# Latent attentions with scores taken on the latent keys and an output projection in split format

## The reference

```
q_c = rmsnorm(h @ w_qa, g_qa)                     # 128 tokens x 192
q = (q_c @ w_qb) -> 32 heads x (128 + 64)         # q_nope, q_rope
kv = h @ w_kva;  k_c, k_rope = kv[:64], kv[64:]   # 64 latent values, 64 rotary values
k_c = rmsnorm(k_c, g_kva)
k_nope, v = (k_c @ w_kvb) -> 32 heads x (128 + 128)
q_rope, k_rope = rotary(q_rope), rotary(k_rope)   # k_rope is the same for all heads
scores = ([q_nope, q_rope] . [k_nope, k_rope]) * (128 + 64) ** -0.5
out = concat_heads(softmax(scores) @ v) @ w_o     # 4096 x 512
```

## Time and profile before

| | us |
|---|---|
| median of 3 executions | 1812.53 |
| lowest, highest | 1809.76, 1815.47 |
| the profiled execution, its own time | 1815.04 |
| its span, first to last instruction | 1813.2 |

### The profile page before, as it was taken

One profiled execution on the slowest core, in us unless ns is written; L12 is line 12 of the kernel. 1 busy time (PEld: TensorE's weight loads), 2 busy tenths in 40 slices (PEclk: granted clock), 3 DMA queues, 4 the chain that ended last, 5 costly groups with the idle time before them and its releaser, 6 DMA issues. The chain is left out here.

```text
span 1813.2 us, 23109 instructions
## 1 busy us (share of the span) xinstructions
PE 1622.6 (89%) x7617; PEld 1207.7 (67%) x7617; DVE 1071.5 (59%) x2144; ACT 890.5 (49%) x1528; POOL 207.4 (11%) x186
## 2 busy tenths in 40 slices
PE   5999999999987568797899987978999999999995
PEld 4778877887853233574666655756777777877873
DVE  5566666576649941443478844435665665575473
ACT  4554555455444311232188862326565565565552
POOL 0000000000013500000156640000000000000000
PEclk9999999999999868899999988999999999999997
DMA  7010011101090033253342103532010010010011
GB/s 265 1 58 35 27 54 54 39 23 58 2 361 24 0 157 92 79 168 116 71 87 38 27 7 114 168 142 113 1 59 35 23 58 35 31 50 35 23 54 73
DMA packets 30248, 129.51 MB, mean 71 GB/s; under 512 B 4929, under 2 KB 7105, under 8 KB 21489
## 3 DMA queue, kind: packets, MB, share of 16 engines
q1 hardware_dynamic: 30192, 128.84, 21.5%
HBM read 123.06 MB, written 0.26 MB: 68 GB/s over the span
## 5 line engine op out<-in xcount | busy, mean ns | idle before, releaser
L1871 POOL TENSOR_TENSOR L2x_p_lo<-L2x_e_t,L2x_p_hi 128x512 fp32r<-128x512 f32 x80 | 105.1, 1325 | 62.8 <-ACT L2x_p_hi L2056 61.9
L746 DVE TENSOR_TENSOR L0x_k_lo<-bank,L0x_k_hi 128x512 fp32r<-128x512 f32 x128 | 85.7, 689 | 42.6 <-ACT L0x_k_hi L635 42.2
L746 DVE TENSOR_TENSOR L3x_k_lo<-bank,L3x_k_hi 128x512 fp32r<-128x512 f32 x128 | 85.5, 689 | 40.0 <-ACT L3x_k_hi L635 39.8
L389 PE MATMUL bank<-L0x_ctx_hi,L0x_w_hi 128*128 128x512 f32 x256 | 103.7, 405 | 4.2 <-DVE L0x_ctx_lo L661 4.2
L389 PE MATMUL bank<-L3x_ctx_hi,L3x_w_hi 128*128 128x512 f32 x256 | 102.9, 402 | 4.2 <-DVE L3x_ctx_lo L661 4.2
L390 PE MATMUL bank<-L3x_ctx_lo,L3x_w_hi 128*128 128x512 f32 x256 | 101.2, 395 | 0.0
L635 ACT ACTIVATE L0x_k_hi<-bank 128x512 fp32r<-128x512 f32 x128 | 74.2, 599 | 54.8 <-PE bank L511 54.8
L391 PE MATMUL bank<-L0x_ctx_hi,L0x_w_lo 128*128 128x512 f32 x256 | 101.1, 395 | 0.0
L391 PE MATMUL bank<-L3x_ctx_hi,L3x_w_lo 128*128 128x512 f32 x256 | 100.9, 394 | 0.0
L635 ACT ACTIVATE L3x_k_hi<-bank 128x512 fp32r<-128x512 f32 x128 | 74.0, 599 | 53.9 <-PE bank L511 53.9
L390 PE MATMUL bank<-L0x_ctx_lo,L0x_w_hi 128*128 128x512 f32 x256 | 100.3, 392 | 0.0
(11 more groups left out here) (618 smaller groups left out, 4229.8 us busy)
## 6 DMA issues: line engine op xcount, KB each, us to landing
L0x_w_kqv<-in_L0x_kqv SPq DMA_DIRECT2D x7, 1536.0 KB, 6.3
L3x_w_kqv<-in_L3x_kqv SPq DMA_DIRECT2D x7, 1536.0 KB, 6.3
L0x_w_o<-in_L0x_o SPq DMA_DIRECT2D x8, 1024.0 KB, 4.9
L1a_w_o<-in_L1a_o SPq DMA_DIRECT2D x8, 1024.0 KB, 4.8
L2a_w_o<-in_L2a_o SPq DMA_DIRECT2D x8, 1024.0 KB, 5.0
L3x_w_o<-in_L3x_o SPq DMA_DIRECT2D x8, 1024.0 KB, 4.9
L0x_s<-in_ctx_t SPq DMA_DIRECT2D x4, 1024.0 KB, 12.2
L0a_w<-in_L0a_w SPq DMA_DIRECT2D x4, 1024.0 KB, 10.9
```

Of the source, the lines that this page charges most:

```text
L389: pe.matmul(out, left[0], right[0], start=start, stop=False)
L746: dve.tensor_tensor(p_lo[:, kt % 4, :], ring_bank(kt)[:], bits(p_hi[:, kt % 4, :]), ALU.subtract).then_inc(p_ready, 1)
L1871: pool.tensor_tensor(p_lo[:, t % 8, :], e_of(t), bits(p_hi[:, t % 8, :]), ALU.subtract).then_inc(low_pool, 1)
```

## The change

Scores. The key projection is gone. Instead each head's query (128 rows) is multiplied by that head's key weights (`w_kb`, a new tile, 128 rows by the 64 latents, written twice side by side), `absorb`, L2325's place taken by matmuls into bank 1; the result's 64 rows and the 64 rows of the turned rotary queries are copied into one tile `qk_t` of 128 rows, and the score is one matmul per head against `kc_t`, which holds the 64 key latents and the 64 rotary key values. So that the copies stay in their own rows, even heads have latents first and odd heads rotary first; `kc_t` exists in both orders.

Output projection. The values weighed are kept as `o_hi` (fp32r, by ScalarE) and `o_lo` (the rest, by VectorE); the weights as `wo_hi` (ScalarE, `split_high`, four copies per group) and `wo_lo` (GpSimd, `split_low`, four subtractions per group). For each head three fp32r matmuls replace one in full fp32. All groups add up in bank 4; x is added to once, at the end. The addition into x in each step and its wait go.

Order. On TensorE the value projection comes behind weighing, then the rotary transposes (now into the free half of bank 3), then `absorb`, then the output projection. On VectorE `o_lo` comes behind the rotary addition, then the copies of the turned and the absorbed halves, and the probabilities' multiplication last. On ScalarE `split_high(g+1)` comes last in a step and waits for `project_out(g-1)`. The load of w_o waits for `wo_lo` two groups back instead of for the projection.

```diff
+                sp.dma_start(w_kb[b][:], a["kb"][b]).then_inc(w_in[b], 16)
...
+                def split_low(g, b):
+                    for h in range(HG):
+                        pool.wait_ge(wo_hi_ready, g * 4 + h + 1)
+                        pool.tensor_tensor(wo_lo[b][:, h, :], w_o[b][:, h, :], bits(wo_hi[b][:, h, :]),
+                                           ALU.subtract).then_inc(wo_lo_ready, 1)
...
                 def load_output(n, b):
-                    sp.wait_ge(wo_done, n - 1)
+                    sp.wait_ge(wo_lo_ready, n * 4 - 4)
...
-                    pe.wait_ge(k_copied, g + 1)
-                    for h in range(HG):
-                        mm = pe.matmul(banks[1][:, h * P:(h + 1) * P], w_lo[b][:, KO + h * HD:KO + (h + 1) * HD],
-                                       lat_lo[:, 1, :], start=True, stop=True)
-                    mm.then_inc(k_proj, 1)
...
+                def absorb(g, b):
+
+                    pe.wait_ge(q_copied, g + 2)
+                    pe.wait_ge(qk_copied, g + 1)
+                    for h in range(HG):
+                        mm = pe.matmul(banks[1][:, h * P:(h + 1) * P], w_kb[b][:, h, :], q_t[:, h, :],
+                                       start=True, stop=True)
+                    mm.then_inc(absorbed, 1)
+
                 def score(g):
...
-                        pe.matmul(banks[5][:, h * P:(h + 1) * P], q_t[:, h, :], k_t[:, h, :], start=True, stop=False)
-                        mm = pe.matmul(banks[5][:, h * P:(h + 1) * P], q_pe_t[:, h, :], lat_lo[:, 2, :],
-                                       start=False, stop=True)
+                        mm = pe.matmul(banks[5][:, h * P:(h + 1) * P], qk_t[:, h, :], kc_t[:, h % 2, :], start=True,
+                                       stop=True)
...
+                def project_out(g, b, first=False, last=False):
+                    pe.wait_ge(o_lo_ready, g + 2)
+                    pe.wait_ge(wo_lo_ready, g * 4 + 4)
                     for h in range(HG):
-                        mm = pe.matmul(banks[6][:], o_t[:, h, :], w_o[b][:, h, :], start=(h == 0),
-                                       stop=(h == HG - 1))
+                        pe.matmul(wo_bank[:], o_hi[:, h, :], wo_hi[b][:, h, :], start=(first and h == 0), stop=False)
+                        pe.matmul(wo_bank[:], o_hi[:, h, :], wo_lo[b][:, h, :], start=False, stop=False)
+                        mm = pe.matmul(wo_bank[:], o_lo[:, h, :], wo_hi[b][:, h, :], start=False,
+                                       stop=(last and h == HG - 1))
...
                     if after:
+                        project_v(g + 1, 1 - b)
                         turn_rotary(g + 1)
+                        absorb(g + 1, 1 - b)
                     if before:
-                        project_out(g - 1, 1 - b, prev_i)
+                        project_out(g - 1, 1 - b, first, last)
...
+                def split_high(g, b, i, used=True):
+                    act.wait_ge(o_in[b], i * 16 + 16)
+                    if used:
+                        act.wait_ge(wo_done, g - 1)
+                    for h in range(HG):
+                        act.activation(wo_hi[b][:, h, :], w_o[b][:, h, :], ACT.Copy).then_inc(wo_hi_ready, 1)
...
                     if after:
                         keep_v(g + 1, 1 - b, used=before)
+                    if before and further:
+                        split_high(g + 1, 1 - b, i)
...
                     if after:
-                        keep(g + 1)
+                        keep_rotary(g + 1)
+                    if before:
+                        dve.wait_ge(o_hi_ready, g)
+                        dve.tensor_tensor(o_lo[:], per_head(banks[7]), bits(o_hi[:]), ALU.subtract).then_inc(o_lo_ready, 1)
+                    if after:
+                        keep_turned(g + 1)
+                        keep_absorbed(g + 1)
...
-                    if before:
-                        dve.wait_ge(wo_done, g)
-                        dve.tensor_tensor(core.x[:], core.x[:], banks[6][:], ALU.add).then_inc(x_added, 1)
...
+                dve.wait_ge(wo_done, NG)
+                dve.tensor_tensor(core.x[:], core.x[:], wo_bank[:], ALU.add)
```

More of the change, by code:

```diff
@@ L2224, in latent_attention @@
         p_t = st.sb("p_t", [P, HG, P])
-        o_t = st.sb("o_t", [P, HG, P])
+        o_hi = st.sb("o_hi", [P, HG, P], F32R)
+        o_lo = st.sb("o_lo", [P, HG, P], F32R)
+        wo_hi = [st.sb(f"wo_hi{b}", [P, HG, D], F32R) for b in range(2)]
+        wo_lo = [st.sb(f"wo_lo{b}", [P, HG, D], F32R) for b in range(2)]
         own = st.sem("own")
@@ L2399, in _ @@
                 step(NG - 1, 1, NG // 2 - 1, after=False)
-                step(NG, 0, NG // 2, this=False, after=False)
+                step(NG, 0, NG // 2, this=False, after=False, last=True)
             @block.scalar
@@ L2415, in _, with keep_q @@
                 act.activation(rstd[:, 1:2], sumsq[:, 1:2], ACT.Sqrt, bias=bias, scale=1.0 / KR).then_inc(rms_ready, 1)
-                def keep_q(g):
+                def keep_q(g, used=True):
                     act.wait_ge(q_proj, g + 1)
-                    if not (isinstance(g, int) and g == 0):
-                        act.wait_ge(s_ready, g)
+                    if used:
+                        act.wait_ge(absorbed, g)
                     act.activation(q_t[:], per_head(banks[0]), ACT.Copy).then_inc(q_copied, 1)
@@ L2427, in keep_v, with step @@
                     act.activation(v_sb[b][:], per_head(banks[2]), ACT.Copy).then_inc(v_copied, 1)
-                def step(g, b, before=True, this=True, after=True):
+                def step(g, b, i, before=True, this=True, after=True, further=True):
                     if before:
                         act.wait_ge(p_turned, g)
+                        if not (isinstance(g, int) and g == 1):
+                            act.wait_ge(o_ready, g - 1)
                         act.activation(p_t[:], per_head(banks[6]), ACT.Copy).then_inc(p_t_ready, 1)
@@ L2441, in step @@
                         act.wait_ge(o_ready, g)
-                        act.activation(o_t[:], per_head(banks[7]), ACT.Copy).then_inc(o_t_ready, 1)
+                        if not (isinstance(g, int) and g == 1):
+                            act.wait_ge(wo_done, g - 1)
+                        act.activation(o_hi[:], per_head(banks[7]), ACT.Copy).then_inc(o_hi_ready, 1)
                     if after:
                         keep_v(g + 1, 1 - b, used=before)
-                keep_q(0)
+                    if before and further:
+                        split_high(g + 1, 1 - b, i)
+                keep_q(0, used=False)
+                split_high(0, 0, 0, used=False)
                 keep_v(0, 0, used=False)
-                step(0, 0, before=False)
-                with act.Fori(0, NG // 2 - 1) as i:
-                    step(i * 2 + 1, 1)
-                    step(i * 2 + 2, 0)
-                step(NG - 1, 1, after=False)
-                step(NG, 0, this=False, after=False)
+                step(0, 0, 0, before=False)
+                split_high(1, 1, 0, used=False)
+                step(1, 1, 1)
+                step(2, 0, 1)
+                with act.Fori(1, NG // 2 - 1) as i:
+                    step(i * 2 + 1, 1, i + 1)
+                    step(i * 2 + 2, 0, i + 1)
+                step(NG - 1, 1, 0, after=False, further=False)
+                step(NG, 0, 0, this=False, after=False, further=False)
             @block.vector
@@ L2476, in _ @@
-                steps.then(dve.tensor_tensor(k_sw[:, 0:half], src[:, half:], rot[:, 1, 0:half], ALU.mult))
+                dve.scalar_tensor_tensor(lat[:], banks[0][:, 0:QR], rstd[:, 0:1], row_sb[:, 0:QR],
+                                         ALU.mult, ALU.mult)
+                for order in range(2):
+                    dve.scalar_tensor_tensor(kc[:, order, order * KR:(order + 1) * KR], banks[0][:, QR:QR + KR],
+                                             rstd[:, 1:2], row_sb[:, QR:], ALU.mult, ALU.mult)
@@ L2484, in keep, with keep_rotary @@
+                def keep_rotary(g, used=True):
                     dve.wait_ge(pe_proj, g + 1)
[L2485 removed]
+                    if used:
                         dve.wait_ge(pe_turned, g)
[L2487 to L2488 removed]
+                    wide, thin = [P, HG // 2, RD], [P, HG // 2, half]
                     cos = rot[:, 0, :].unsqueeze(1).to_broadcast(wide)
@@ L2510, in turn_rotary, with keep_absorbed @@
                     copy.then_inc(pe_copied, 1)
+                def keep_absorbed(g):
+                    dve.wait_ge(absorbed, g + 1)
+                    for odd in range(2):
+                        rows = slice(odd * RD, (odd + 1) * RD)
+                        copy = dve.tensor_copy(qk_t[rows, odd:HG:2, :], per_head(banks[1])[rows, odd:HG:2, :])
+                    copy.then_inc(qk_copied, 1)
                 def step(g, b, before=True, this=True, after=True):
```

140 lines of the change are left out of this document (74 added, 66 removed).

## The result

| | before, us | after, us |
|---|---|---|
| median (lowest to highest), 4 runs each | 1811.78 (1809.76 to 1815.47) | **1780.89** (1777.76 to 1782.18) |
| profiled execution, its own time | 1815.04 | 1777.76 |
| its span | 1813.2 | 1776.0 |
| mean granted TensorE clock | 0.955 | 0.958 |

The ratio is 0.9824, with an interval of 0.981 to 0.9838: the change makes the kernel 1.8% faster, 30.9 us. The forecast was 1782. The changed kernel was timed twice more, five executions each time, against before on the same chip: 1776.93 (0.9817, interval 0.9794 to 0.984) and 1776.6 (0.9811, 0.9787 to 0.9834).

What follows compares the result with a forecast made beforehand. TensorE was taken as the bound, its steady step falling 2.31 us to 9.65. Steady steps 27.7, first steps 0.8, tails 3.0 and clock -1.0 sum to 30.5 us off: median 1782, range 1769 to 1797.

Steps and rivals of the forecast that it cites:

- Output projection: TensorE, each step: 4 full fp32 matmuls become 12 fp32r passes taking 2.75 us, 0.78 less.
- The gap: TensorE ahead of the output projection: 0.7 us of waiting and issue goes, as o_hi and o_lo are hidden.
- The ring: Closed chain from projection through ScalarE's split, exponentials, o_hi and o_lo to projection: 9.15 us, 0.45 to spare, cost 0.
- Rival A: The ring through ScalarE is the bound: 0.5 to 1 us more a step, 1791 us; chance 0.18.
- GpSimd's hold: VectorE's rotary addition held at worst for one GpSimd instruction, 1.33 us: 0 in steady steps, 0.6 in each stage's first.
- Rival C: VectorE is kept out for GpSimd's whole run: step 10.6 us, at 6 us held 13.8 and 1834 in all; chance 0.05.
- First step: First to second score in each latent stage: 8.11 us becomes 7.0 to 7.1, gain 1.0 minus 0.6 for the hold.
- Tail: Eighth score to the end of the last addition into x: 16.25 us against 17.78, 1.5 less per stage.
- clock -0.5 a stage: Tails of both latent stages: 0.5 us lost in each to TensorE's lower clock, bounds -1.7 to +2.75.
- Preparation: Ahead of the first score: key projection goes, absorb and its copies come, 0 within 1 us per stage.
- Rival B: TensorE's sum as forecast, edges free, L1a's clock regained, passes at 0.221 us: 1777 us; chance 0.17 with the forecast's scatter.
- D: The change does not do what it says: within 5 us of the time before; chance 0.03.

Runs made afterwards that it cites:

- e1: Changed kernel with the output projection back in full fp32, without the split of weights and values: 1781.02 us, run again 1782.17 us.
- e3: Changed kernel with the value projection back ahead of weighing on TensorE: 1791.39 us (one execution).
- e4: Two runs of the changed kernel, with one or two more ScalarE copies of 128x512 behind each group's four: 1788.46 and 1786.11 us (one execution each).
- e5: Changed kernel with GpSimd's four subtractions per group cut from 128x512 to 128x4: 1774.86 us, ratio 0.9799.
- e8: Kernel before the change, with all groups added up in one PSUM bank and x added to once at the end: 1815.46 us (one execution).
- e4_act_plus2: Changed kernel with two more ScalarE copies of 128x512 behind the four of each group: 1786.11 us (one execution).
- e6: Changed kernel with GpSimd's four subtractions of 128x512 issued as one of 128x2048: 1797.39 us, ratio 0.9905.
- e7: Changed kernel with ScalarE's order changed in the last steps and VectorE's multiplication moved earlier in the first step: 1777.54 us, ratio 0.9801.
- e2: Changed kernel with every score matmul issued twice: 1793.64 us (one execution).

## Why the prediction was right, step by step

- *The bound.* TensorE's sum, right: doubling the scores lengthened the step by exactly their 0.90. Forecast 9.65 with the edges, measured 9.62 in L1a. In L2a the six steps came to 9.81 on average (1095.71 to 1154.54), because of the late second step.
- *Scores.* 0.89 less, right (773.10 to 773.99). Keys for absorb, 0: right within 0.01 (absorb 0.90 in e1).
- *Output projection.* 2.75 forecast; absorb and projection take 3.66, less 0.90 is 2.76. Right. Its gain was split wrongly: 0.67 by e1, not 0.78, because 3.53 held 0.10 of restart after the wait. The removed gap is worth that much more, 0.8 instead of 0.7. The sum of both is the same.
- *The gap.* Hidden, right: no wait in steady steps, and e3 brings 0.62 of it back. The chain from weighing to the projection was put at 1.6 of 1.98, a spare of 0.38; e3 gives 0.24.
- *The ring.* 9.15 with 0.45 of slack, right by e4. That the sum fits so closely is in part luck: in the step shown the exponentials take 1.54 (1.64 forecast), the output projection behind its short wait 2.87 (2.75), and the rest differs by less than 0.1. Rival A (the ring is the bound) is excluded, by a margin of less than one copy.
- *GpSimd's hold.* "Until that one instruction has ended": right for both lengths. The addition ends 0.28 us behind the end of one subtraction in both, and takes 1.54 beside instructions of 1.28 and 3.87 beside one of 4.52. Rival C (kept out for the whole run) is excluded: held to the end of the four (779.24) and 0.28 more, the addition would have taken 2.9. The step's cost of 0 was right (e5). The 0.6 per stage for the held multiplication was the mean of a thing that either does not happen or costs 1.16 us in the step behind it. The SBUF page of the Trainium skill ("SBUF — State Buffer", section "Who interferes with whom") says that a VectorE instruction with two SBUF inputs contends with a GpSimd instruction that reads SBUF, and calls the shared ports an exclusive lock. The traces agree: the addition of 0.43 took 3.87 beside the subtraction of 4.52, which had started 0.93 ahead of it.
- *First step.* 7.0 to 7.1 forecast, 6.94 and 6.93 measured: right.
- *Tail.* 16.25 forecast, 16.16 in L1a (811.53 to 827.69), right. In L2a 17.76, of which 1.6 is the stretch at the lower clock. The term "clock -0.5 a stage" was 0 in L1a, and L1a gave back the 1.7 that before had lost there (-3.3 instead of -1.5), which the sum had not counted; in L2a it was 1.6. A mean of 0.5 stood for a cost that is there or not.
- *Preparation.* 0 within 1: 0.3 and 0.7 gained, within the bound; e8 shows that the stretch in L2a moves by 1.1 without a change of its code. *DMA.* w_o landed in 7.1 us, not 4.8, beside more traffic; nothing waited for it.
- *Sum.* Steady steps 26.9 (27.7 forecast), first steps 2.35 (2.0, less 1.2 for the hold, which is in the steady steps here), tails 3.3 (3.0 less 1.0 for the clock), preparation 1.0 (0): 33.6 against 30.5. The terms that were too small are L1a's tail and the preparation (1.3 and 1.0), and the steps by 0.7 together. The medians of the three timings are 30.9, 33.8 and 35.2 us below before's on the same chip; the forecast was 30.5. That the first of them comes within 0.4 is luck as far as it is closer than the terms: in the profiles the stages gave 3 us more than the sum, and executions of one kernel differ by more than that.

Rival B (the forecast with free edges, 1777) differs from the forecast in the edges and in 0.1 us a step for the passes, which did not come (0.230 each, not 0.221). At the edges both are seen: the profile with neither a hold nor the lower clock in the two stages took 1772.9, those in which one stage has both 1777.76 and 1775.15, and the medians of the second and third timing, 1776.93 and 1776.6, are B's. D is excluded by every row.

Not settled: what makes a tail, or L0f, run at the lower clock in one execution and not in the next, and so whether the forecast or B is nearer to the kernel's usual time.

## What to carry to other kernels

When TensorE's timeline is closed (no waits in it), as it was here, a matmul saved is time saved, and the work that replaces it on other engines is free as long as each closed ring (here projection, split, exponentials, o_hi, o_lo, projection) adds up to less than TensorE's sum: add the ring up before building, and remember its slack, here half a microsecond. Give GpSimd short instructions beside VectorE operations that read two SBUF tensors; the hold is one instruction, so its length sets the price. Price the slot of a matmul that follows a wait apart from its restart, or one edit is credited with another's gain.

## What the runs showed of the hardware

- VectorE and GpSimd meet in both directions. Where VectorE's multiplication went first, a GpSimd subtraction took up to 1.82 us instead of 1.28. Which one goes first differed between the two stages of one execution, with starts that agree to 0.01 us. VectorE gets its turn between two subtractions although the next is due.
- One GpSimd subtraction of 128x2048 takes 4.52 us where four of 128x512 take 5.17.
- Twelve fp32r passes of 512 columns take 2.76 us, 0.230 each, also when they add up over eight groups in one bank; the same product in full fp32 takes 3.43, 0.858 a matmul. At the lower clock a pass takes 0.43.
- Tails after steps with idle time on TensorE (e3, e4_act_plus2, e6) were 16.9 to 19.5 us, while those of e1 (two profiles) and of e7, whose steps are closed, agree to 0.01. In e2 the steps from the third score on had no idle time either and the tails were still 16.7 and 18.2, so idle steady steps alone don't explain it; e2 did have the held multiplication in both stages.
- The changed kernel's executions on one chip scatter by 4 to 9 us, before's by 5 to 11, and part of it is seen in the profiles as stages with two lengths: L0f with L1x (3.4 us) and each latent stage of the changed kernel (2.7 us, 103 or 105.6 to 106.1). An edit worth less than these has to be read from its stage, not from the total.
